# One step order of a five-engine layer loop: output turns, normalisation, band copy and norms moved

## What is computed

```python
for i in range(6):
    x = attn_layer(shift_tokens(x), Wqkv[i], q_scale[i], k_scale[i], Wo[i]) + x
    x = ffn_layer(shift_tokens(x), ln_g[i], ln_b[i], W1[i], b1[i], W2[i], b2[i]) + x
# attn_layer, 16 heads of 64, windows of 32 tokens that look one window back:
    q, k, v = split(x @ Wqkv)
    q, k = l2norm(q) * qs, l2norm(k) * ksc        # then rotary tables: x * cos + swapped x * sin
    sim = einsum(q, k of this window and the one before) * 8, masked
    out = softmax(sim) @ v                        # then out @ Wo
# ffn_layer:
    xn = layernorm(x) * g + bln
    a, gate = split(xn @ W1 + b1)
    return (a * gelu(gate)) @ W2 + b2
```

## Time and profile before

| | us |
|---|---|
| median of 3 runs | 2338.65 (2337.27 to 2339.2) |
| the profiled execution | 2337.19 |
| its span | 2335.4 |
| PE busy | 2159.0 (92%) |
| ACT busy | 1738.4 (74%) |
| DVE busy | 1489.0 (64%) |
| POOL busy | 1365.7 (58%) |

### The profile page before, as it was taken

One profiled execution on the slowest core, in us unless ns is written; L12 is line 12 of the kernel. 1 busy time (PEld: TensorE's weight loads), 2 busy tenths in 40 slices (PEclk: granted clock), 3 DMA queues, 4 the chain that ended last, 5 costly groups with the idle time before them and its releaser, 6 DMA issues.

```text
span 2335.4 us, 66376 instructions
## 1 busy us (share of the span) xinstructions
PE 2159.0 (92%) x22450; PEld 1523.6 (65%) x22450; DVE 1489.0 (64%) x3344; ACT 1738.4 (74%) x4329; POOL 1365.7 (58%) x1541
## 2 busy tenths in 40 slices
PE   4799999999999999999999999999999688969999
PEld 2366666666666666666666666666666356649998
DVE  6667777677776776767767677677776366651111
ACT  2588888888888888888888888888888455534444
POOL 2787777777777777777777777777776121200000
PEclk7899999999999999999999999999999799979999
DMA  2222232222322223222232222322222200000000
GB/s 73 57 65 60 50 88 60 60 60 50 88 60 60 60 50 88 60 59 61 49 87 60 59 61 49 87 61 59 62 49 59 73 2 1 0 1 3 4 4 7
DMA packets 156775, 119.49 MB, mean 51 GB/s; under 512 B 45806, under 2 KB 148660, under 8 KB 156596
## 3 DMA queue, kind: packets, MB, share of 16 engines
q1 hardware_dynamic: 156724, 118.82, 21.3%
HBM read 23.28 MB, written 1.05 MB: 10 GB/s over the span
## 4 chain that ended last, share of the span: by engine, by line
PE 59%; ACT 13%; DVE 12%; issue 7%; POOL 7%; DVEq 0%; POOLq 0%; ACTq 0%
PE bank L598 7%; PE bank L565 6%; PE bank L539 5%; PE bank L1411 5%; PE bank L1402 5%; PE bank L505 4%; PE bank L579 4%; PE bank L478 4%; ACT pr L666 4%; PE bank L507 3%; POOL sqh L819 3%; POOL kr L816 3%; PE bank L468 3%; PE bank L460 2%; DVE t L724 2%
## 5 line engine op out<-in xcount | busy, mean ns | idle before, releaser
L666 ACT ACTIVATE pr<-bank,mx 128x64 f32<-128x64 f32 x1536 | 335.5, 342 | 16.6 <-DVE mx L746 16.6
L723 DVE TENSOR_TENSOR t<-bank,rot_t 128x512 f32<-128x512 f32 x384 | 262.5, 684 | 86.5 <-PE bank L505 82.5
L807 POOL TENSOR_TENSOR qr<-qr,rn 128x512 f32<-128x512 f32 x192 | 199.5, 1039 | 187.8 <-DVE rn L706 187.8
L751 DVE TENSOR_REDUCE ss<-sqh 128x16 f32<-128x512 f32 x192 | 131.7, 686 | 266.6 <-POOL sqh L819 266.6
L813 POOL TENSOR_TENSOR qr<-t 128x512 f32<-128x512 f32 x192 | 245.3, 1278 | 86.9 <-DVE t L724 86.9
L628 ACT ACTIVATE sq<-bank 128x512 f32<-128x512 f32 x192 | 114.6, 597 | 213.1 <-DVE t L724 211.8
L724 DVE TENSOR_TENSOR t<-bank,rot_t 128x512 f32<-128x512 f32 x384 | 261.5, 681 | 0.0
L816 POOL TENSOR_TENSOR kr<-t 128x512 f32<-128x512 f32 x192 | 245.1, 1277 | 0.3 <-DVE t L724 0.3
L819 POOL TENSOR_TENSOR sqh<-sq 128x512 f32<-128x512 f32 x192 | 243.8, 1270 | 0.4
L565 PEld LDWEIGHTS bank<-kBD,qT 128*32 128x32 f32 x6144 | 156.1, 109 | 116.6 <-issue 115.7
L674 ACT ACTIVATE kBD<-bank 64x512 f32<-64x512 f32 x384 | 228.7, 596 | 3.1 <-PE bank L487 0.8
(11 more groups left out here) (172 smaller groups left out, 4549.3 us busy)
## 6 DMA issues: line engine op xcount, KB each, us to landing
vBD<-vS SPq DMA_DIRECT2D x1152, 64.0 KB, 2.0
vBD<-vS SPq DMA_DIRECT2D x576, 32.0 KB, 1.9
wqkv<-in_L_ffn_Wqkv_dram SPq DMA_DIRECT2D x12, 768.0 KB, 6.4
wo<-in_L_ffn_Wo_dram SPq DMA_DIRECT2D x12, 256.0 KB, 2.8
vBD<-in_L_ffn_W_dram SPq DMA_DIRECT2D x1, 2048.0 KB, 9.3
w<-in_L_ffn_W_dram SPq DMA_DIRECT2D x6, 341.0 KB
const<-in_const_dram SPq DMA_DIRECT2D x1, 1158.0 KB, 5.2
out_dram<-acc SPq DMA_DIRECT2D x8, 128.0 KB, 1.8
```

The source lines that it names most:

```text
L666: ins = act.activation(pr[:, slot % 2, hd, :], bank[5][:, hd * 64:(hd + 1) * 64], ACT.Exp, bias=mx[:, slot % 2, hd:hd + 1])
L723: dve.tensor_tensor(t1[:, m], src, tab[:, 0, :].unsqueeze(1).broadcast_to([P, HH, DH]), ALU.mult)
L807: pool.tensor_tensor(x, x, rn[:, slot, half * HH:(half + 1) * HH].unsqueeze(2).broadcast_to([P, HH, DH]), ALU.mult).then_inc(norm.sem, 1)
```

## The change

Seven edits, all in the order of statements or the place of a wait:

- PE: the transposes of the outputs stand behind v in all steps, where before they did in step 0 alone.
- PE: the q matmul of step 0 waits only for the first product of the feed-forward (bank 0), and the k matmul for the second (bank 1), where q waited for all three.
- ACT: the band copy for step 0's scores is made at the head of step 0, not at the head of step 4. In step 4 the load of the gelu table is then the first instruction.
- ACT: the square of k stands ahead of the copy attT.
- DVE: the maximum of the scores stands ahead of the moments of the layer norm (step 2).
- DVE: the normalised outputs ob stand ahead of the sums of squares (and of the residual, which only step 0 has).
- POOL: in step 1 the two scalings with the norms stand ahead of the shifted copy lns.

The gelu table's own statement has not been moved.

```diff
                         if live(3):
-                            pe.wait_ge(h_mul.sem, h_mul.after(i - 3))
+                            pe.wait_ge(h_mul.sem, h_mul.after(i - 3, 1))
...
                     pe.wait_ge(k_sq.sem, k_sq.after(n - 1))
+                    if j == 0 and live(3):
+                        pe.wait_ge(h_mul.sem, h_mul.after(i - 3, 2))
                     pe.matmul(bank[1][:, :], xt, wqkv[:, INNER + h * 512:INNER + (h + 1) * 512],
...
-                if has(F_O) and j:
-                    _, slot, n = unit(F_O)
...
-                    mm.then_inc(ot_mm.sem, 1)
...
-                if has(F_O) and j == 0:
+                if has(F_O):
...
             for i, j, live, has, unit in units(act):
-                if j and live(1):
+                if j < UPB and live(1) and (j or live(2)):
                     act.wait_ge(p_exp.sem, p_exp.after(UPB * (i - 1) + j - 1))
                     seed(j % NT)
...
+                if has(F_Q):
+                    _, _, n = unit(F_Q)
+                    act.wait_ge(k_mul.sem, k_mul.after(n))
+                    act.activation(sq[:, HH:, :], bank[1][:, :].rearrange("p (h d) -> p h d", d=DH), ACT.Square).then_inc(k_sq.sem, 1)
                 if has(F_O):
...
-                if j == 2 and live(2):
-                    ln_moments(dve, i - 2)
                 if has(F_S):
...
+                if j == 2 and live(2):
+                    ln_moments(dve, i - 2)
+                if has(F_P):
+                    _, slot, n = unit(F_P)
+                    par = slot % 2
+                    dve.wait_ge(o_mm.sem, o_mm.after(n))
+                    dve.wait_ge(p_inv.sem, p_inv.after(n))
...
             for i, j, live, has, unit in units(pool):
-                if j == 1 and live(2):
-                    m = i - 2
-                    pool.wait_ge(u_res.sem, u_res.after(2 * m + 1))
-                    pool.wait_ge(ln_t1.sem, ln_t1.after(m - 1))
-                    hold(pool)
-                    shifted_copy(pool, lns, m & 7, ln_part, m).then_inc(ln_in.sem, 1)
```

More of the change, by code:

```diff
@@ L638, in layers_act @@
                                    bank[4][:, :].rearrange("p (a b) -> p a b", a=HP), ACT.Copy).then_inc(ot_ev.sem, 1)
[L639 to L642, removed]
                 if has(F_Q):
@@ L747, in layers_dve @@
                                       negate=True).then_inc(s_max.sem, 1)
+                if j == 2 and live(2):
[5 more added lines that the diff above has]
+                    dve.wait_ge(p_inv.sem, p_inv.after(n))
+                    dve.tensor_tensor(ob[:, par], bank[7][:, :].rearrange("p (h d) -> p h d", h=HH),
+                                      rinv[:, par, :].unsqueeze(2).broadcast_to([P, HH, DH]), ALU.mult).then_inc(o_norm.sem, 1)
                 if has(F_Q):
@@ L757, in layers_dve @@
                                              op0=ALU.add, op1=ALU.add).then_inc(f_res.sem, 1)
[L758 to L764, removed]
                 if has(F_O) and unit(F_O)[1] % NT == NT - 1:
@@ L808, in layers_pool @@
                                            ALU.mult).then_inc(norm.sem, 1)
+                if j == 1 and live(2):
+                    m = i - 2
+                    pool.wait_ge(u_res.sem, u_res.after(2 * m + 1))
+                    pool.wait_ge(ln_t1.sem, ln_t1.after(m - 1))
+                    hold(pool)
+                    shifted_copy(pool, lns, m & 7, ln_part, m).then_inc(ln_in.sem, 1)
                 if has(F_Q):
```

## The result

| | before | after |
|---|---|---|
| median of 4 runs, us | 2338.43 (2337.27 to 2339.2) | 2296.93 (2294.76 to 2301.1) |
| profiled execution, its span | 2337.19, 2335.4 | 2294.76, 2293.0 |
| one turn of the loop | 36.44 | 35.54 |

The ratio is 0.9825, 95% interval 0.9808 to 0.9842. The change makes the kernel 1.75% faster, where 2279 against 2338.65 would have been 2.55%. The predicted 2279 was 18 us too low, and the range held the time. The turn says it more sharply than the time: 0.90 us won where 1.29 was forecast. 44 turns give 39.6 of the 42.4 us between the two profiled executions; the other 2.8 lie outside them. The kernel before was run 17 more times beside the experiments: one of these runs was slow, with 4312.65 us, and is left out everywhere, and the others took 2336.5 to 2349.6.

What follows compares the result with a forecast made beforehand. PE, busy 35.17 of 36.45 us, was taken as the bound; pieces of 12.16, 8.88, 5.69 and 8.38 plus 0.04 made a turn of 35.15, gaining 1.29 over 44 turns, plus 3 us: 2338.65 - 60 = 2279 us, range 2258 to 2303.

Steps and rivals of the forecast that it cites:

- D: PE's stretch from q of step 1 to the product with v of step 2: 12.72 to fall to 12.16 us.
- A: PE's stretch from step 2's product with v to step 4's transposes: 9.30 to fall to 8.88 us.
- The wait for lnk: Step 2, v's weight load in its new place waits for ACT's copy lnk: charged 0.10 us, bounds 0 and 0.3.
- The chain through DVE and ACT: From step 2's product with v through ob, sums, products and copies to the exponentials: 8.88 us, setting A.
- the waits of 0.66 and 0.58: PE's waits for ob in step 2 (0.66 us) and for kBD in step 3 (0.58), both claimed to go.
- Piece B: PE's stretch from the transposes of step 4 to q of step 0: 6.24 to fall to 5.69 us.
- The meeting of norms and turn of k: Step 4: norms ready 7.50 us after the output projection, PE's path 7.53, so a wait of 0 to 0.1.
- Piece C: PE's stretch from q of step 0 to q of step 1: 8.18 to 8.38 us, new wait for attT 0.20.
- a drain: Rival, chance 0.04: a table-switch drain of about 1380 ns delays pT in step 4; turn about 36.2, 2327 us.
- PE as the only bound: Rival, chance 0.10: the chain of 8.88 is shorter and neither new wait appears; turn about 34.5, 2249 us.
- The late DVE chain: Rival, chance 0.17: step 2's products start only 0.6 us earlier, attT about 0.4 late; gain 0.85 a turn, 2298.
- the slower rival: Rival, chance 0.04: attT behind the square of k delays the turn of k in steps 2 and 0; 36.6, 2346 us.

Runs made afterwards that it cites:

- run 17: Not a label: the unchanged kernel before was run 17 more times; one took 4312.65 us and is left out, the others 2336.5 to 2349.6.
- experiment 5: Changed kernel with only the transposes of the outputs put back ahead of v in steps 2 to 4: 2296.28 us, turn 35.40.
- experiment 3: Changed kernel with DVE's sums of squares of step 2 moved behind the rotary products of step 3: 2292.0 us, turn 35.58.
- experiment 7: Changed kernel with ob put back behind the sums of squares on DVE: 2293.22 us, turn 35.53.
- experiment 9: Kernel before with one edit alone, POOL's two scalings with the norms ahead of lns in step 1: 2280.57 us, turn 35.09.
- experiment 11: Changed kernel with the moments of the layer norm ahead of the maximum again in step 2: 2292.61 us, turn 35.54.
- experiment 1: Changed kernel with the norms made ahead of step 3's residual uT on DVE: 2278.03 us, turn 34.98.
- experiment 6: Changed kernel with the band copy put back at the head of step 4: 2295.84 us, turn 35.57.
- experiment 10: Changed kernel with q of step 0 waiting for all three products of the feed-forward again: 2294.21 us, turn 35.59.
- experiment 2: Changed kernel with the copy attT ahead of the square of k again, in step 0 only: 2280.67 us, turn 35.22.
- three more edits: Changed kernel with the edits of experiment 1, experiment 2 and experiment 3 together: 2252.39 us, ratio to before 0.9618, turn 34.56.
- experiment 8: Changed kernel with POOL's scalings put back behind the copy lns in step 1: 2327.29 us, turn 36.12.

## Why the prediction came out as it did

**Pieces D and A** were right to 0.03 us: 12.13 against 12.16 and 8.87 against 8.88. The wait for lnk that was charged with 0.10 is there (0.13, experiment 5). DVE's first product of step 2 starts 1.07 after q instead of 2.61, which is the 1.5 of the prediction. The chain through DVE and ACT is there: experiments 3 and 7 shorten it and shorten A, and in the changed kernel the turned probabilities of step 4 start 0.04 after the exponentials end.

**What failed in them is the credit.** The prediction let v's cover take the waits of 0.66 and 0.58 away. The runs show that POOL's edit takes both alone (experiment 9), and that v's new place costs 0.13 in step 2. The maximum's place, which was to make v's cover in step 3 enough, changes nothing beside the others (experiment 11). The prediction also took the terms of the chain of 8.88 as given. The 0.60 for the sums stands in it only because the change puts them there. No edit was costed alone; had that been done, the chain with ob last would have come out at an estimated 8.28, under PE's own path of 8.72, and the edit on ob as a loss.

**Piece B** is the term that failed: 5.69 forecast, 6.05 measured. It is 0.36 too short and makes up most of the 0.39 by which the turn was forecast too short. The meeting of norms and turn of k was worked out nearly right: 7.50 and 7.53, "a wait of 0 to 0.1". The measured distance is 7.56, which is the 7.50 and 0.06 until PE starts, and the wait 0.11. PE's own path is 7.46 (experiment 1), not 7.53: the sum took 0.44 from the turn of k to q, where the trace of before has 0.49 in step 4. What was missing is what that small wait does behind it. It stands at the end of the loop's body, and q of step 0 follows 0.81 after the turn of k, where before it was 0.49: another 0.32. The up projections won 0.63 and not 0.55, which takes 0.08 off again. Where the loop ends, the next turn (47) is written out and PE does not jump back. There the same wait is ahead of the turn of k, and q follows at 0.49:

```profile
1715.95 0.66 PE L478 MATMUL bank<-const,qr 128*128 128x128 f32 x4
1716.56 0.66 PE L487 MATMUL bank<-const,kr 128*128 128x128 f32 x4
1717.05 1.05 PE L505 MATMUL bank<-wqkv,xs 128*128 128x512 f32 x2
```

The kernel of experiment 3 has a wait of 0.19 in that place and the same 0.49. Without the wait but with the jump back it is 0.43 (experiment 1) to 0.55 (experiment 6). So neither comes with 0.3 by itself; both together do. One reading fits but is not shown: the sequencer of PE, which hands it its instructions, usually runs ahead and takes the jump and the loop's wait instructions under the matmuls, and a wait just before takes the lead away. The trace has no view of that lead, only "issue". Turn 47 also lacks the register instructions of the loop's steps, and no run parts these from the jump. That the split wait isn't the cause is shown (experiment 10).

**Piece C** was 8.49 for 8.38, and the new wait 0.28 for 0.20. The chain to the turn of k is 4.99 us instead of 4.91, because PE started 0.15 after attT ended (1046.95 against 1046.21 + 0.59) and not 0.05; the rest is 0.03 in small starts. The mechanism was right, and experiment 2 gives back 0.31.

**The rivals.** By the Trainium skill (ScalarE: Activation LUTs, What ACT_TABLE_LOAD costs) a switch has a drain of about 1380 ns beside its load of about 1283 ns. The drain does not show here either: the copy starts 1.30 us after the load does, and the load takes 1.28.

```profile
1036.48 1.28 ACT L612 ACT_TABLE_LOAD   x1
1037.78 0.60 ACT L621 ACTIVATE pT<-bank 128x512 f32<-128x512 f32 x1
```

PE as the only bound did not come about (35.54, not 34.5), but three more edits bring 34.56. The late DVE chain would have given almost the measured time, 2298, for a reason that was not there. A time within the range is thus no proof of its cause. Its mechanism, which is also that of the slower rival, appears when POOL's edit is taken out (experiment 8), at a price of 0.58 in step 2 beside the 0.28 in step 0, and the turn of 36.12 stays under 36.44: the two waits are together under the 1.5 us from which the slower rival decides.

## What to carry to other kernels

Cost each edit of a bundle alone and with one left out. Here one of seven gave more than all seven, since others of them lengthened the chains in pieces A and C and laid a wait open in D. Where waits for two different tiles go back to one late producer, move the producer first. A wait of "0 to 0.1 us" at the end of a loop's body deserves its own price. So do gains ahead of a wait that hangs on something else: here they were given back, as in experiments 3, 6 and 7.

## What the runs showed of the hardware

In the hardware loop, a wait of PE of 0.11 to 0.19 us ahead of the last matmul group of a turn came with a start of the next turn's first group 0.81 after it in the mean. Without the wait it is 0.43 to 0.55. With the wait, but where the loop ends and PE goes on into written-out code, it is 0.49. That was not expected, and its cause stays open.

PE started 0.05 us after the copy or the exponentials of ACT that it waited for ended (pT in experiment 6: 1038.92, 1038.97), but 0.15 where the turn of k waited for attT (step 0 of the changed kernel, step 2 in experiment 8).
